# A further wait ahead of the gathers of a graph aggregation: GpSimd also waits for TensorE's sums of the step three back

## The reference, cut to what matters

```
for each head:                                      # layer 0
    e     = leaky_relu(s[row] + d[col], 0.2)        # one number for each edge
    ex    = exp(e - m[row])
    alpha = ex / segment_sum(ex, row)[row]
    out   = segment_sum(alpha[:, None] * hW[col], row)
```

## Time and profile before

| | us |
|---|---|
| median of 3 runs | 6628.58 (6621.03 to 6629.74) |
| the profiled execution | 6631.88 |
| its span | 6630.1 |
| aggregation of layer 0, first gather to end of the last | 494.5 to 2531.6 |
| aggregation of layer 1, first gather to end of the last | 3384.5 to 5416.9 |
| POOL busy, whole span | 3464.2 (52%) |
| DVE busy, whole span | 4374.5 (66%) |
| PE busy, whole span | 4948.0 (75%) |

### The profile page before, as it was taken

One profiled execution on the slowest core, in us unless ns is written; L12 is line 12 of the kernel. 1 busy time (PEld: TensorE's weight loads), 2 busy tenths in 40 slices (PEclk: granted clock), 3 DMA queues, 4 the chain that ended last, 5 costly groups with the idle time before them and its releaser, 6 DMA issues. The chain is left out here.

```text
span 6630.1 us, 90296 instructions
## 1 busy us (share of the span) xinstructions
PE 4948.0 (75%) x21196; PEld 3538.8 (53%) x21197; DVE 4374.5 (66%) x8953; ACT 1782.7 (27%) x4856; POOL 3464.2 (52%) x3669
## 2 busy tenths in 40 slices
PE   1456667776767664699767777777778877999999
PEld 1345555555555552466444444455555546666665
DVE  8987787887888778622566666667676666333333
ACT  7322232232233233222320000012222215333332
POOL 0117777777777774144147777777777754000000
PEclk8678888888888886799888888888787778999999
DMA  1012222222222222322455455455555543000001
GB/s 59 16 41 58 57 57 56 58 56 57 58 56 58 57 57 66 114 64 64 135 151 139 139 139 139 137 140 149 147 146 145 146 113 84 5 5 9 5 5 39
DMA packets 380643, 534.45 MB, mean 81 GB/s; under 512 B 119263, under 2 KB 240118, under 8 KB 380406
## 3 DMA queue, kind: packets, MB, share of 16 engines
q0 software_dynamic: 139648, 299.92, 18.9%
q1 hardware_dynamic: 240886, 233.29, 11.6%
HBM read 475.96 MB, written 56.96 MB: 80 GB/s over the span
## 5 line engine op out<-in xcount | busy, mean ns | idle before, releaser
L876 POOL DMA_INDIRECT got<-table,st_idx x3232 | 3084.5, 954 | 1012.4 <-issue 916.7
L952 PE MATMUL ps_sum<-weighted,hot 128*128 128x260 f32 x6464 | 1851.9, 445 | 173.7 <-DVE acc L1024 168.9
L952 PEld LDWEIGHTS ps_sum<-weighted,hot 128*128 128x128 f32 x6464 | 1387.5, 226 | 589.3 <-DVE acc L1024 257.7
L1024 DVE TENSOR_TENSOR acc<-acc,ps_sum 128x260 f32 x1664 | 707.0, 425 | 752.0 <-PE ps_sum L952 616.9
L937 PE MATMUL ps_score<-score_split,hot_t 128*128 x3232 | 246.7, 184 | 981.5 <-DVE z L1004 955.3
L1016 DVE TENSOR_TENSOR weighted<-got,ps_weight 128x2048 f32<-128x2048 f32 x404 | 921.5, 2281 | 4.3 <-ACT weighted L912 0.8
L937 PEld LDWEIGHTS ps_score<-score_split,hot_t 128*128 128x128 bf16 x3232 | 191.4, 100 | 1162.6 <-issue 1144.7
L909 ACT ACTIVATE ps_weight<-z 128x32 f32<-128x32 f32 x404 | 81.2, 201 | 2657.0 <-DVE z L1004 2657.0
L3058 DVE SCALAR_TENSOR_TENSOR x_res<-ps_yf,comb,x_res 128x256 f32 x392 | 189.7, 484 | 638.0 <-PE ps_yf L2966 638.0
L975 DVE TENSOR_TENSOR hot<-ps_score,row_loc 128x1024 f32<-128x1024 f32 x404 | 492.0, 1218 | 3.5
L2946 PE MATMUL ps_hf<-acc,ws_f 128*128 (+2 forms) x896 | 348.2, 542 | 6.0 <-ACTq L2993 6.0
(11 more groups left out here) (533 smaller groups left out, 7384.4 us busy)
## 6 DMA issues: line engine op xcount, KB each, us to landing
spread<-row_list SPq DMA_DIRECT2D x404, 256.0 KB
got<-table,st_idx POOLq DMA_INDIRECT x3232, 2.8
gate_xin<-ball_rows SPq DMA_DIRECT2D x98, 128.0 KB, 2.3
got_y_e<-y_rows SPq DMA_DIRECT2D x10, 896.0 KB
table<-row_e SPq DMA_DIRECT2D x50, 130.0 KB, 2.4
ball_rows<-xt SPq DMA_DIRECT2D x10, 640.0 KB, 4.7
mix_xin<-ball_rows SPq DMA_DIRECT2D x49, 128.0 KB, 2.0
xn_rows<-xs_m SPq DMA_DIRECT2D x49, 128.0 KB, 1.7
```

What stands on the lines that cost most here:

```text
L876: pool.indirect_dma_start(got[:, r, k, :], None, table, bass.IndirectOffsetOnAxis(ap=st_idx[:, r, k:k + 1], axis=0))\
L952: last = nc.tensor.matmul(ps_g[:, p % 2, 0:AW], hot[:, r % 2, k, :], weighted[:, r % 2, k, :], start=(k == n * p), stop=(k == n * p + n - 1))
L1024: nc.vector.tensor_tensor(acc[:, ds(b * AW, AW)], acc[:, ds(b * AW, AW)], ps_g[:, p % 2, 0:AW], ALU.add).then_inc(added, 1)
```

## The change

The gathers of step `j` get one more condition. It is left out for the first three steps. For step `j` the count `first_entry(j - 2)` is reached when the last sum of step `j - 3` is made.

```diff
                 pool.wait_ge(idx_staged, j + 1)
                 if not first:
                     pool.wait_ge(scaled, j - (STEP_RING - 1))
+                if not first or r >= 3:
+                    pool.wait_ge(summed, first_entry(j - 2))
                 if not first or r > 1:
                     t, q = (turn, r - 2) if r > 1 else (turn - 1, STEP_RING + r - 2)
                     pool.wait_ge(gathered[q], t * (16 * (KT - 1)) + 16 * (KT - 1))
```

## The result

The changed kernel takes 6899.93 us (median of 4 runs, 6890.29 to 6911.14), the kernel before 6627.12 (4 runs on the same chip, 6621.03 to 6629.74). The ratio is 1.0415, with an interval from 1.0403 to 1.0427. The forecast was 6785, in a range from 6710 to 6860: right in sign and place, but 115 us short.

The account below looks back on a forecast made before the run. GpSimd's gathers were taken to set the pace of the two aggregations. Stalls of 35 (layer 0), 61 and 60 us (layer 1's halves) sum to 156, on 6631.9 giving 6788, less 3.3 for the median: 6785, range 6710 to 6860.

Parts of the forecast that it names:

- where the wait closes a loop: Aggregations: from L993 of step i + 1 to step i's sum, to step i + 3's gather, to its L993.
- the reaction: GpSimd after a true wait: gather starts 0.86 us after the sum's end; ends taken as 0.30 and 0.95.
- a sum keeps its distance to its L993: Rule for carrying shifts forward in both aggregations: time from L993 to a step's sum stays as before; total 156 us.
- three kinds of even steps: Layer 1, first half: 17, 15 and 17 steps, losing 0, 1.0 and 2.8 us each, 62.
- rival of the clock: TensorE's clock falls further as stalls leave it idle: 117 us more, 6902, half of that 6843; chance 0.16.
- its distance to its gathers: Both aggregations: L993 keeps its distance to its gathers or the L993 before; last loop leg 11.66 us.
- the 61: Layer 1, first half: 33 stalls costing 61 us.
- 60: Layer 1, second half: 46 stalls costing 60 us.
- upper price of 6902: Clock rival with all sums slow: 137 instead of 61 in layer 1's first half, 76 instead of 35 in layer 0.
- slow already: Layer 1, second half: odd steps' high sums already slow, even ones with 2 us to spare; argued against the clock rival.
- The test that I set for it: Layer 1's two windows: forecast wrong if granted clock differs by more than 0.05 from 0.83 and 0.79.
- The rival of full clock: Layer 1's high sums run at 2.4 GHz, loop 19.6 under 20.1, no stall left, 6624; chance 0.05.

Follow-up runs that it names:

- the larger filler: 72 unread matmuls in the loop's steps of layer 1 and 32 in the others, added to the changed kernel: 6697.2 us, ratio 1.0108.
- The late load: Changed kernel with SyncE's 256 KB load of `spread` in layer 1 waiting for `z` of step i - 3: 6842.82 us, ratio 1.0334.
- without the load's collision: Changed kernel with both the 72 (32) filler matmuls and the `spread` load waiting for `z` in layer 1: 6674.2 us, ratio 1.0073.

## Why the prediction was wrong, point by point

**Right: what bounds, and where the wait closes a loop.** The gathers set the pace, the wait instruction is free, only the high half's sum matters, the reaction is 0.78 to 0.86 us, and outside the aggregations nothing changed. Layer 0 was forecast at 35 us and gave 27.6 in the profile, 25 by leaving it out.

**Wrong: "a sum keeps its distance to its L993".** This is the step that failed. The forecast carried over into the changed kernel three kinds of even steps: 17 at 6.9, 15 at 8.6 and 17 at 10.3 us from L993 to the sum's end. Those are two clocks of TensorE. In the changed kernel the fast kind is gone. Of 48 even steps 1 is under 8 us, 25 stand at 8.6 on average and 22 at 10.95. The 17 steps that should have had no stall have one, and thus all 49 odd steps do. In the second half the steps over 9.5 us went from 9 to 35 of 48. The granted clock within the leg fell from 0.80 to 0.63 in the first half and from 0.695 to 0.61 in the second. Two stretches of the kernel before show what that means for one leg (columns as in the earlier trace rows), and a third, of the changed kernel, is the leg of the loop shown above:

```profile
3949.36:3960.34 10.98, 9.28 (x23) 5.24 (x24) 4.79 (x10) 1.09 (x5) 8.24 (x10) 0.56 0.53 145
3909.20:3916.09 6.89, 5.15 (x23) 3.12 (x24) 4.81 (x10) 1.09 (x5) 5.36 (x6) 1.00 0.60 172
...
3937.62:3948.63 11.01, 9.28 (x23) 5.25 (x24) 4.80 (x10) 1.09 (x5) 5.56 (x6) 0.54 0.35 98
```

The same 23 matmuls, 9.28 us busy near 1.2 GHz and 5.15 at 2.4. And the guest's matmul between 3420 and 4400 us (all or most of layer 1's first half), ns of one (min/median/max), in the kernel before, in the changed one, and in the changed one with the larger filler:

```profile
L2492 PE MATMUL ps_gate_mix<-wkv,gate_xin x192: 592/863/1193, 3430.0 to 4376.0; 128*128 128x512 f32 x192
```

```profile
L2494 PE MATMUL ps_gate_mix<-wkv,gate_xin x168: 592/1061/1202, 3442.2 to 4383.2; 128*128 128x512 f32 x168
```

```profile
L2497 PE MATMUL ps_gate_mix<-wkv,gate_xin x184: 592/592/1154, 3446.6 to 4384.9; 128*128 128x512 f32 x184
```

The cause is a feedback. A late gather makes `z` late, TensorE stands idle for it (359.9 us in the first half, which takes 1123 us, against 268.0 in 1011), it starts `score`, the guest's piece and the high sums at 1.2 GHz, the sums end later, and the next gather with them:

```profile
PE ps_score L939 <- DVE z L1006: 359.9, 96, 17.9
```

```profile
PE ps_score L937 <- DVE z L1004: 268.0, 99, 17.8
```

The Trainium skill ("TensorE: Matmul & The Clock Gate", section "HAM oscillation — how this bites in real kernels") describes a loop in which each wait for data sends the clock back down, so that every short group of matmuls begins slow. The 0.63 of this leg agrees. The prediction cited that passage for its rival of the clock and gave it 0.16. In its own sum every leg kept the clock that it had.

Priced: the leg's excess is 1.05 x 49 = 51 us in the first half and 0.71 x 47 = 33 in the second. That it is the clock, and not something else on the leg, is shown by the larger filler: with it the leg falls below even its old length, and 200 us go.

**Missed: the landing leg.** The forecast kept L993 at "its distance to its gathers". In the first half that leg grew from 1.98 to 2.64 us, 0.66 x 49 = 32 us, since the broadcast load now falls on the last gathers. The late load shows it.

**The sum again.** First half: 61 + 51 + 32 - 4 (a reaction of 0.78 for 0.86) = 140, measured 137. That is a little too neat: the 61 counts the fast steps at nothing where their loop was 0.6 us short of 20.1, and from the averages of the table it is 56, while the gathers' 0.08 x 49 = 4 are left out. Second half: 60 + 33 + 4 (gathers and landing, 9.81 + 1.94 for 11.66) = 97, measured 105. Layer 0: 35 forecast, 28 measured. The rest, 239 less the two halves, is some -2 at the stage's ends. Together 156 became 267.

**The rival of the clock** was the right one at 0.16, and its upper price of 6902 is near the measured 6900. That is partly luck. It had every stall at 2.8 us in the first half, which is what came (140 us, forecast 137), though a quarter of that is the landing leg's; it gave 41 us more to layer 0, where the cost fell instead, and nothing to the second half, where the odd steps' sums were held to be "slow already" and still lost 0.71 us each.

**The test that I set for it was too coarse.** The prediction would be wrong, it said, if the windows' clock moved by more than 0.05 from 0.83 and 0.79. It moved to 0.80 and 0.75, inside that bound, while the clock of the leg in the loop fell by 0.17. In the first half the even steps' clock fell as the odd steps' rose, 0.80 to 0.88, and the mean hid both.

**The rival of full clock** held that at 2.4 GHz no stall would be left and the time would be 6624. With the larger filler it is 6697, and 6674 without the load's collision. The first is wrong by the landing leg (2.96 us there) and by what remains in layer 0 and at the ends. By layer 1's aggregation, 2307.9 us goes to 2116.4 with the clock up, to 2085.2 with the load moved too, and stands 30 above its base of 2054.8. So of the 239 us that layer 1 lost, 178 hang on TensorE's clock (192, of which 14 were there to be had in the kernel before), 31 on the load, and 30 stay with the clock up. The 178 are more than the 84 above, since the filler also speeds up the legs that were slow before the change, which the forecast had counted. Layer 0's 29 come on top, but no filler stood there, so they aren't a price at full clock.

**Open:** how much of layer 0's 25 to 28 us is clock wasn't tried, since no filler stood there, nor was the load moved there. Nor is it shown why the second half's leg lost less clock than the first's (0.085 against 0.17), nor what the 30 us of layer 1 are that stay, beyond the stall at its start.

## What to carry to other kernels

A wait that closes a loop through TensorE must be priced with TensorE's clock after the change: before carrying over a distribution of durations, ask which of its kinds the new idle time will turn into the slow one. Look at the granted clock within the leg that is in the loop, step kind by step kind, not at a stage's mean. And ask of every transfer that a starved engine releases early, what it now lands on.

## What the runs showed of the hardware

- GpSimd's gathers run 0.30 us apart as long as the counts that they wait for are reached in time, and a fourth such wait costs nothing (ratio 0.9999). After a true wait on a semaphore the gather starts 0.78 to 0.86 us after the end of the sum that releases it. The Trainium skill ("DMA: Bandwidth & Descriptors", section "Anatomy of one DMA — SWDGE (gpsimd) path") gives some 50 ns for a dispatch and some 100 ns for a semaphore update. The latency in this trace is over five times their sum, so these two don't make it up.
- More matmuls made the kernel faster: 21008 instructions more in the trace (111698 against 90690, weight loads included), and 200 us less. In the first half 32 filler matmuls, which ended over 5 us before `score`, did nothing for the clock of the leg, and 72 did.
- A 256 KB load by one queue stretched the landing of the last gathers on another by 0.7 us on average (2.64 us for 1.98, and 1.88 with the load moved), in a stage that moves less than it did: 123 GB/s, against 139 before.
